# Both additions of a state group on GpSimd, in two of the eight groups of a step

## What is computed

```
proj = layernorm(x) @ in_proj_w;  x, z = split(proj)
xc   = silu(conv4(x))                       # per channel, 4 taps
dt_r, B, C = rmsnorm of xc @ x_proj_w.T     # 64, 16 and 16 wide
dt   = softplus(dt_r @ dt_proj_w.T + dt_bias)
h[d, n]_t = exp(dt[d]_t * A[d, n]) * h[d, n]_(t-1) + dt[d]_t * B[n]_t * xc[d]_t
y[d]_t    = sum over 16 n of h[d, n]_t * C[n]_t  +  D[d] * xc[d]_t
out = (y * silu(z)) @ out_proj_w.T
```

## Time and profile before

| | us |
|---|---|
| median of three runs | 5033.81 |
| the profiled execution | 5034.98 |
| its span | 5033.2 |
| TensorE matmul busy | 4636.0 (92%) |
| VectorE busy | 4508.3 (90%) |
| GpSimd busy | 3919.6 (78%) |
| ScalarE busy | 3573.8 (71%) |

### The profile page before, as it was taken

How to read it: one execution, slowest core, us unless ns; L and a number is a source line. 1 busy time by engine, 2 the same in 40 slices (tenths; PEclk the granted TensorE clock), 3 DMA queues, 4 the chain that set the end, 5 groups by cost and what they waited for, 6 DMA issues and landing times.

```text
span 5033.2 us, 73049 instructions
## 1 busy us (share of the span) xinstructions
PE 4636.0 (92%) x22816; PEld 3960.4 (79%) x22816; DVE 4508.3 (90%) x7793; ACT 3573.8 (71%) x8734; POOL 3919.6 (78%) x2218
## 2 busy tenths in 40 slices
PE   5688899999999999999999999999999999998886
PEld 4566778888788888888888888888888888886676
DVE  2599999999999999999999999999999999998940
ACT  2577777777777777777777777777777777777720
POOL 0488888888888888878788887878888888888830
PEclk8888999999999999999999999999999999998997
DMA  4423224343433434343343534334343434333222
GB/s 155 170 77 140 103 98 168 121 170 120 172 125 119 178 120 172 118 169 120 127 170 120 178 120 167 122 132 157 128 170 121 176 120 142 139 120 126 90 102 78
DMA packets 158436, 682.05 MB, mean 136 GB/s; under 512 B 18912, under 2 KB 27744, under 8 KB 108896
## 3 DMA queue, kind: packets, MB, share of 16 engines
q1 hardware_dynamic: 139616, 643.82, 35.9%
q10 hardware_dynamic: 18432, 33.56, 1.7%
HBM read 622.26 MB, written 55.05 MB: 135 GB/s over the span
## 4 chain that ended last, share of the span: by engine, by line
POOL 53%; PE 19%; issue 18%; DVE 4%; DMA 3%; ACT 2%; POOLq 0%; SPq 0%; DVEq 0%; ACTq 0%
POOL dbx L349 33%; POOL half L357 17%; PE gx L521 4%; PE g L554 4%; PE ys L447 3%; PE ys L537 3%; PE g L437 3%; DVE hb L931 2%; POOL dtx L392 2%; DMA bb<-bc_scratch 2%; DVE hc L946 1%; PE ys L478 1%; POOL x L372 1%; ACT hb L700 1%; DVE gx L985 1%
## 5 line engine op out<-in xcount | busy, mean ns | idle before, releaser
L931 DVE TENSOR_TENSOR_SCAN hb<-hb,hstate,dbx 128x256 f32<-128x256 f32 x4096 | 2844.9, 740 | 139.7 <-ACT hb L700 83.5
L349 POOL TENSOR_TENSOR dbx<-dtx,bb 128x1024 f32<-128x1024 f32 x1024 | 2414.6, 2358 | 446.1 <-DVE hb L931 350.4
L700 ACT ACTIVATE hb<-dt,a_neg 128x256 f32<-128x256 f32 x4096 | 1789.5, 468 | 66.5
L357 POOL TENSOR_TENSOR half<-hc 128x512 f32<-128x512 f32 x1024 | 1300.3, 1270 | 303.1 <-DVE hc L946 271.8
L946 DVE TENSOR_TENSOR hc<-hb,cb 128x512 f32<-128x512 f32 x2048 | 1379.9, 674 | 0.0
L447 PE MATMUL ys<-half,ident 128*128 128x256 f32 x4096 | 1110.8, 396 | 182.6 <-POOL half L357 182.3
L447 PEld LDWEIGHTS ys<-half,ident 128*128 128x128 f32 x4096 | 767.9, 195 | 344.0 <-POOL half L357 225.9
L537 PE MATMUL ys<-xnT,wz 128*128 128x256 f32 x4096 | 965.8, 391 | 62.4 <-DVE ybuf L966 59.0
L554 PE MATMUL g<-ybuf,wo 128*128 128x256 f32 x4096 | 1008.5, 391 | 5.3 <-DVE x L992 4.7
L537 PEld LDWEIGHTS ys<-xnT,wz 128*128 128x128 f32 x4096 | 785.9, 196 | 199.4 <-issue 95.4
L521 PE MATMUL gx<-xnT,wx 128*128 128x256 f32 x4096 | 940.0, 384 | 2.3 <-issue 2.3
(11 more groups left out here) (59 smaller groups left out, 2407.1 us busy)
## 6 DMA issues: line engine op xcount, KB each, us to landing
wx<-in_win SPq DMA_DIRECT2D x128, 1024.0 KB, 4.8
wz<-in_win SPq DMA_DIRECT2D x128, 1024.0 KB, 4.8
wo<-in_wout SPq DMA_DIRECT2D x128, 1024.0 KB, 5.0
wf<-wf_scratch SPq DMA_DIRECT2D x128, 512.0 KB, 3.3
xc_scratch<-xcn ACTq DMA_DIRECT2D x128, 256.0 KB, 2.0
xcs<-xc_scratch SPq DMA_DIRECT2D x128, 256.0 KB, 5.1
bb<-bc_scratch SPq DMA_DIRECT2D x64, 512.0 KB, 7.4
cb<-bc_scratch SPq DMA_DIRECT2D x64, 512.0 KB, 6.5
```

Source lines behind the costliest of these rows:

```text
L349: nc.gpsimd.tensor_tensor(dbx[:, k % 2, :].rearrange("p (n t) -> p n t", n=NQ), dtx[:, a * T:(a + 1) * T].unsqueeze(1).to_broadcast([P, NQ ...
L357: nc.gpsimd.tensor_tensor(half[:, k % 4, :], hc[:, k % 2, 0:HALF], hc[:, k % 2, HALF:GW], ALU.add).then_inc(halves, 1)
L700: ins = nc.scalar.activation(h[:, m * T:(m + 1) * T], dt[:, j % 2, a * T:(a + 1) * T], ACT.Exp, scale=a_neg[:, ds((2 * j + a) * N + 2 * v ...
L931: ins = nc.vector.tensor_tensor_scan(h[:, m * T:(m + 1) * T], h[:, m * T:(m + 1) * T], dbx[:, k % 2, (2 * w + m) * T:(2 * w + m + 1) * T], ...
```

## The change

Group k = 1 and group k = 5 are the second group of each half (k % 4 == 1). For them GpSimd makes the first addition as before, waits for its own result on a new semaphore, and adds the two 256-column parts of `half` in place. TensorE then adds one product with the identity in place of two. The six other groups stay as they were. In every step there are two more GpSimd additions of 128x256, two more waits of GpSimd on itself, and two fewer products on TensorE.

```diff
+        pair_sums = sem("pair_sums")
...
             def group_sum(S, k):
                 pool.wait_ge(hcs, after(UNITS * S + 2 * k + 2))
                 pool.wait_ge(sum_mm, after(8 * S + k - 3))
-                nc.gpsimd.tensor_tensor(half[:, k % 4, :], hc[:, k % 2, 0:HALF], hc[:, k % 2, HALF:GW],
+                both = nc.gpsimd.tensor_tensor(half[:, k % 4, :], hc[:, k % 2, 0:HALF], hc[:, k % 2, HALF:GW],
+                                               ALU.add)
+                if k % NQ != 1:
+                    both.then_inc(halves, 1)
+                    return
+
+                both.then_inc(pair_sums, 1)
+                pool.wait_ge(pair_sums, after(2 * S + k // NQ + 1))
+                nc.gpsimd.tensor_tensor(half[:, k % 4, 0:T], half[:, k % 4, 0:T], half[:, k % 4, T:HALF],
                                         ALU.add).then_inc(halves, 1)
...
                         pe.wait_ge(halves, after(8 * SG + k + 1))
-                        for i in range(2):
+                        for i in range(1 if q == 1 else 2):
                             mm = nc.tensor.matmul(ys[a][:, 0:T], ident[:], half[:, k % 4, i * T:(i + 1) * T],
```

## The result

The changed kernel takes 5057.63 us, the median of five runs (5057.2 to 5065.0), against 5033.81 us before: a ratio of 1.0051 with a 95% interval of 1.0037 to 1.0066. It is slower by 23.8 us, where 34 us were forecast. The profiled execution is the slowest of the five, 5065.0 us with a span of 5063.2 us, so it stands 7 us above its own median. Its span is 30.0 us longer than the one before.

What follows compares the result with a forecast made beforehand. A loop through VectorE, GpSimd, TensorE and ScalarE was taken to set the ordinary step. Fifteen chunks at +1.91 us (+28.7) plus +5.4 in the last gave 34 us on 5034.98, 5069; less 1.2 for the median, 5068 us, range 5036 to 5110.

Steps and rivals of the forecast that it cites:

- The loop: Scan 12, GpSimd sum 5 to sum 7, TensorE to dt_proj, ScalarE exponentials, next scan 12: sets the ordinary step, 34.43 us.
- the first step: First step of a chunk: its waits come from TensorE, so the saved product shortens it by 0.43 us.
- A: GpSimd time added per changed group: 0.69 us second addition plus 0.21 us wait, 0.90 us; bounds 0.60 and 1.44.
- The self-wait: GpSimd waiting on its own first sum before the second addition: 0.17 us of waiting, 0.21 us more than no wait.
- The ordinary step: Group 5's addition adds 0.90 us, group 1's saved product takes off 0.43: +0.47 us, five in a chunk +2.35.
- The step before the last: Step of a chunk whose length VectorE sets with the norm's statistics; only the late dbx 0 counts, +0.21 us.
- The last chunk: TensorE waits for sum 2, so group 1's addition counts too and no saved product does: about +0.9 us in six steps, +5.4.
- The last step: Last step of a chunk, ended by TensorE: +0.21 us for dbx 0, less 0.43 for group 1's product, -0.22 us.
- The first chunks: Chunks at the start, with less TensorE work, taken as equal to the others at +1.91 us each.
- A (TensorE's relief decides): Rival: GpSimd's additions vanish in its idle time and saved products shorten steps; 21 us less, 5013 us; chance 0.08.
- B: Rival: TensorE has play between sum 7 and dt_proj, only dbx 0 counts; 6 us slower, 5040 us; chance 0.10.
- C (falls in ordinary steps): Rival: longer idle ahead of sum 7 lowers TensorE's clock, 2.9 us a step, 189 us, 5257 us; chance 0.06.

Runs made afterwards that it cites:

- group 1 alone: Only group 1 gets both additions on GpSimd and one TensorE product, group 5 as before; against the kernel before: 4995.03 us, 0.9926.
- The additions alone: Changed kernel, but TensorE still adds both parts in groups 1 and 5, so the second part counts twice; 5106.1 us, 1.0143 to the kernel before.
- group 5 alone: Only group 5 gets both additions on GpSimd and one TensorE product, group 1 as before; against the kernel before: 5102.12 us, 1.0133.
- the first four experiments: Against the kernel before: whole edit in group 1 only 0.9926, in group 5 only 1.0133; in both groups, only the GpSimd additions 1.0143, only the saved products 0.9936.
- groups 1 and 2: Both additions on GpSimd and one TensorE product in groups 1 and 2 instead of 1 and 5; against the kernel before: 4985.51 us, 0.9903.
- the products alone: Kernel before with one product instead of two in groups 1 and 5 and no second addition, that part left out of the sum: 5001.02 us, 0.9936.
- groups 1 to 3: Both additions on GpSimd and one TensorE product in groups 1, 2 and 3; against the kernel before: 5018.52 us, 0.9967.
- group 5's addition behind dtx: Changed kernel with group 5's second addition moved behind dtx, ahead of dbx 0; 5027.27 us, 0.9985 to the kernel before.
- groups by step: Both additions on GpSimd in groups 1, 2, 3 in a chunk's first and last step, group 1 in other steps; 4999.89 us, 0.9925 to the kernel before.

## Why the prediction was right, and where its terms were not

- **The loop was right.** All four stretches of the walk are in the trace after, in their order, with ScalarE's wait for dt_proj unchanged at 0.31 us. Most of the signs that were named came: the second addition 729 ns long, a wait at scan 12 (0.38 us), TensorE's wait at sum 7 (1.71 us where 1.5 was forecast), a step of 34.80 us where 34.9 was said. By its terms the wait at sum 7 would be 0.17 + 0.43 + 0.80 = 1.40. The other 0.3 us come from the stretch behind dt_proj: from dt_proj to the next sum on TensorE it takes 6.63 us before and 6.34 after (medians). `z_in_proj(1)`, which stands there, starts 3.10 us behind dt_proj before and 2.89 after; with group 1 alone it starts 3.53 us behind and the trace names its wait after VectorE's gate. Three signs did not come as said: the second addition starts 0.08 us behind the first (0.17 was said), scan 0 does not wait 0.2 us, and the first step is shorter by 0.20 us, not 0.4.
- **A was 0.80 us, not 0.90.** The duration was exact (0.73 forecast, 0.729 measured). The self-wait was mis-sized: 0.17 us of idle time was taken from dbx 0 behind dtx, but from sum 5's start to its second addition's there are 1.35 us, 1.27 of work and 0.08 of wait. With the next start 0.68 us later this is 2.03 us against 1.23, A = 0.80. The additions alone and group 5 alone each show the same number as growth of the step (34.42 to 35.22 us). The ordinary step is therefore +0.37 by the sum and +0.38 measured.
- **Only group 5's addition and only group 1's product count** in an ordinary step: shown by the first four experiments, in both directions. The Trainium skill, GPSIMD Engine Reference, sections Engine selection and Elementwise — side-by-side cycle accounting, would have had elementwise additions off this engine, and its figure scaled to an estimated 0.56 us. The trace shows 0.73 us, so the fixed part matters at this size. Its advice to use VectorE was not tried: VectorE is busy for 34.24 of 34.28 us once the loop is relieved. Against TensorE's products, GpSimd's additions lose in one group and win in others: groups 1 and 2, with two second additions on GpSimd in each step, are 1% faster.
- **The step before the last** was forecast at +0.21 us for a late dbx 0 and came to +0.13 on average (1.6 in twelve). Its working, A less 0.69 of slack, gives 0.11 with A = 0.80, but that this is near the average is luck. In the timeline dbx 0 ends at 1480.98 and scan 0 starts at 1481.02: handing over takes 0.04 us, not 0.11, and from scan 12 to scan 0 it is 7.93 us against 7.89, only 0.04 more. Ten of the twelve steps are 0.06 us longer; the rest is the two in which the clock fell. The last chunk is likewise 4.3 us longer, where six times 0.80 is 4.8 and 5.4 was forecast. The first step became 0.20 us shorter, not 0.43, with a little more time at the slower level (103.5 us in twelve, from 100.8).
- **The last step is the term that failed.** The sum had -0.22 us for it; it is -1.33. Behind it stands the clock: in the step before, the time at the slower level fell from 45 to 19 us in twelve chunks, from falls in 11 of them to falls in 5. In both kernels a fall at the idle stretch ahead of z_in_proj leaves TensorE behind, and the debt is paid in the last step. In the kernel before, the last step takes 37.9 us in the one chunk without a fall, 38.7 to 39.0 in nine, and 40.4 in the two in which the clock stayed low for longer. After, it takes 38.6 in the three chunks with a fall there and 37.5 in the other nine; the two remaining falls come earlier in the step, behind the wait for sum 7, lengthen that step itself and leave no debt. The last step of the chunk without a fall before (its step before the last is the fourth line of the earlier trace rows), and then, of the kernel after, a step before the last with a fall and the last step behind it:

```profile
1306.00:1343.90 37.90, 36.98 (x196) 31.56 (x195) 34.86 (x63) 31.17 (x81) 30.10 (x19) 1.00 0.33 113
```

```profile
1581.60:1618.60 37.00, 32.81 (x161) 27.91 (x160) 36.61 (x65) 29.03 (x71) 31.11 (x20) 0.95 0.33 116
1618.60:1657.20 38.60, 37.53 (x201) 32.30 (x200) 35.10 (x62) 30.73 (x81) 31.50 (x20) 1.00 0.31 110
```

Between steps without a fall the change is -0.4 us, so of the 16.0 us less in twelve last steps about 4 are the shorter step and 12 the falls. The forecast thought of the clock only as a risk for the worse. Why the falls at that stretch became rarer (11 to 3) is open; TensorE's shorter work ahead of it is no sufficient reason, since with group 1 alone they are 10.
- **The first chunks** were taken as equal to the others. They cost 13.6 us, not 3.8: chunk 1's ordinary steps took 35.7 to 37.3 us before and 37.5 after. The first line of the windows after shows one with the clock at 0.91; before, the clock was low for less of some of them, as in this step of the kernel before:

```profile
578.70:614.40 35.70, 31.96 (x144) 26.84 (x143) 33.96 (x59) 26.10 (x64) 29.94 (x18) 0.95 0.29 105
```

- **The rivals.** A (TensorE's relief decides) is out as a mechanism of this change: the relief exists, 33 us as the products alone show, and beside sum 5's addition too (35.22 to 34.80 us in a step), but there it is smaller than the 0.80 us of that addition. B is out: the play between sum 7 and dt_proj would have let the step stay at 34.5. C (falls in ordinary steps) is real and rare: 3 of 60 steps in chunks 2 to 13, at 1.55 us each, not the 2.9 us of a step in chunk 1. Its mechanism is the one that was named: each of the three, and the two in steps before the last, follows within 1.4 us on a wait of 2.04 to 2.06 us for sum 7. There are ten such waits in chunks 2 to 13, and none of the 62 of about 1.7 us has a fall behind it.

The median was missed by 10 us. Of that, 6 us are the profiled execution's distance from its median (7.4 us, with 1.2 taken from the one before). The other 4 us are what remains of terms that cancel, in sums over the span: last steps -13.4, ordinary steps -5.5 for the smaller A and +4.7 for the falls, first steps +2.8, steps before the last -0.9, chunks 0 and 1 +9.8, chunks 14 and 15 -2.5, the edges +1. That the total is so near is luck in part: the last steps alone would have put it 13 us below the forecast, and the first chunks 10 us above.

## What to carry to other kernels

Look for the loop that closes over a step and cut it into stretches by the starts of its links: here an addition on GpSimd cost its full time inside it, and outside it nothing as long as other work covered it (2.1 us of cover for group 1 in an ordinary step), whatever the busy share of its engine. Before the same edit is made in two places, price each place, since here one was worth -39 us and the other +68. Once the loop is relieved, the next bound is near (VectorE, 0.14 us away), and past that what the runs still won lay in the steps of another kind.

## What the runs showed of the hardware

- A GpSimd instruction that waits for the one just before it starts 0.08 us after its end in one place (second addition) and 0.17 us in another (dbx 0 behind dtx). With a third instruction between them the wait costs nothing (1.23 us from start to start, as without a wait). What makes the two differ is open.
- Whether TensorE's granted clock falls from 1.00 to its lower level, half of it (1.2 of 2.4 GHz), does not follow from the length of the idle stretch ahead alone. At the same idle stretch of the step before the last, in it or just behind it, it fell with 2.49 us in 3 of 12 chunks (changed kernel), with 2.59 us in 11 (groups 1 to 3; in the twelfth it had fallen earlier in the step), with 2.77 in 12 (group 5's addition behind dtx), 2.80 in 11 (before), 2.96 in 8 (groups 1 and 2), and with about 3.24 in 10 (group 1 alone, and groups by step) or 8 (the saved products alone). The Trainium skill, TensorE: Matmul & The Clock Gate, section What's actually happening, says that the gate looks at recent activity on a beat of its own, which a kernel does not start, so that the number of slow matmuls differs from run to run. The 30 us between runs of one kernel, in the order of its clock, agree with that; no run here shows the beat.
- With the idle stretch of the step before the last split in two, falls there became rarer (11 to 7, 8 to 4 and 10 to 7 of 12 chunks), and in all three pairs of executions the time at the slower level in the first steps was longer (by 8, 18 and 10 us in twelve). Whether one follows from the other is open, and with it whether a kernel could keep the gain.
